# Row blocks of a routed expert layer: one slot per block, loaded four at a time, and the experts' output biases added per batch

## The reference, cut to what matters

```python
sh = gelu(einsum('td,sdh->sth', xf, sW1) + sb1[:, None, :])          # 2 shared experts, hidden 512
shared = (einsum('sth,shd->std', sh, sW2) + sb2[:, None, :]).mean(axis=0)
topk_vals, topk_idx = top_k(xf @ rW + rb, 2)                         # 8 experts, 2 per token
w = sum(softmax(topk_vals)[:, :, None] * onehot(topk_idx), axis=1)   # [token, expert], 0 where not chosen
h = gelu(einsum('td,edh->eth', xf, W1) + b1[:, None, :])
y = einsum('eth,ehd->etd', h, W2) + b2[:, None, :]
return shared + einsum('te,etd->td', w, y)
```

## Time and profile before

| | us |
|---|---|
| median of 3 runs | 788.84 (787.33, 788.84, 797.35) |
| the profiled execution, its time | 788.99 |
| its span in the profile | 786.9 |

### The profile page before, as it was taken

The page is one execution under the profiler, slowest core; times in us unless marked ns, Lnnn a source line. Parts: engine busy times, 40 slices in busy tenths (PEclk is TensorE's granted clock), DMA queues, the critical chain, the costliest instruction groups (busy, mean ns, idle before and its releaser), DMA issues.

```text
span 786.9 us, 10406 instructions
## 1 busy us (share of the span) xinstructions
PE 566.9 (72%) x3665; PEld 404.0 (51%) x3665; DVE 363.1 (46%) x1067; ACT 338.1 (43%) x565; POOL 251.2 (32%) x296
## 2 busy tenths in 40 slices
PE   2654552678788869878699882996987696987770
PEld 2213431455355633656436752765874675776660
DVE  4869279616673465645624571226321240133113
ACT  1186574565737556654475140330322242322220
POOL 3204047202351254311613147113322437033231
PEclk9955665689897989987589996999878788969895
DMA  4400000395000000000000102532161402656632
GB/s 125 147 1 1 1 1 0 82 170 195 1 1 1 15 1 0 1 1 1 1 0 1 55 14 69 154 102 67 39 188 43 135 21 100 190 143 182 200 94 80
DMA packets 37763, 51.60 MB, mean 66 GB/s; under 512 B 7097, under 2 KB 27362, under 8 KB 37442
## 3 DMA queue, kind: packets, MB, share of 16 engines
q1 hardware_dynamic: 35218, 45.82, 20.9%
q0 software_dynamic: 2496, 5.15, 1.8%
HBM read 41.28 MB, written 13.86 MB: 70 GB/s over the span
## 4 chain that ended last, share of the span: by engine, by line
PE 44%; DVE 23%; POOL 7%; DMA 7%; ACT 7%; issue 7%; SPq 5%; POOLq 0%; DVEq 0%; ACTq 0%
SPq L427 5%; PE ring_s L850 4%; PE bank_d L760 4%; PE bank_o L880 3%; PE bank_m L682 3%; PE ring_s L652 3%; PE ring_u L747 3%; PE bank_o L866 3%; PE ring_s L844 2%; DMA token_pairs<-y_blk,x_blk 2%; PE bank_o L669 2%; DMA x_blk<-expert_rows 2%; POOL expert_rows L1150 2%; PE bank_r L546 2%; PE ring_u L739 2%
## 5 line engine op out<-in xcount | busy, mean ns | idle before, releaser
L958 ACT ACTIVATE probs<-ring_s 128x512 f32<-128x512 f32 (+1 forms) x192 | 95.5, 524 | 118.6 <-PE ring_s L652 116.9
L1100 POOL TENSOR_SCALAR_AFFINE_SELECT probs<-probs 128x256 f32<-128x256 f32 (+1 forms) x96 | 51.6, 570 | 178.7 <-ACT probs L964 178.7
L652 PE MATMUL ring_s<-qT,kT 64*128 64x128 bf16 (+3 forms) x256 | 64.2, 350 | 49.4 <-ACT probs L958 37.8
L1013 ACT ACTIVATE g_ring<-ring_s,w_blk 128x128 f32<-128x128 f32 x184 | 52.5, 370 | 104.4 <-PE ring_s L850 95.4
L1161 POOL DMA_INDIRECT token_pairs<-y_blk,x_blk x46 | 45.6, 991 | 143.9 <-DVE y_blk L1672 143.1
L964 ACT ACTIVATE probs<-probs 128x2560 f32<-128x2560 f32 x32 | 74.8, 2337 | 0.8
L652 PEld LDWEIGHTS ring_s<-qT,kT 64*128 64x128 bf16 x256 | 16.4, 97 | 93.4 <-ACT probs L958 58.6
L850 PE MATMUL ring_s<-xT_blk,w_blk 128*128 128x128 f32 x368 | 57.0, 305 | 4.3 <-DVE xT_blk L1665 2.6
L682 PE MATMUL bank_m<-pair_sum,oT 128*128 128x64 f32 x256 | 44.0, 327 | 22.2 <-DVE oT L1467 22.2
L1063 POOL TENSOR_TENSOR rstd<-var_eps,neg_half 128x4 f32<-128x4 f32 x24 | 24.9, 1036 | 100.5 <-DVE var_eps L1394 100.4
L850 PEld LDWEIGHTS ring_s<-xT_blk,w_blk 128*128 128x128 f32 x368 | 53.4, 222 | 6.8 <-issue 4.3
(11 more groups left out here) (356 smaller groups left out, 1076.8 us busy)
## 6 DMA issues: line engine op xcount, KB each, us to landing
w_blk<-expert_pack SPq DMA_DIRECT2D x46, 514.0 KB
expert_pack<-in_L_ffn_W SPq DMA_DIRECT2D x16, 256.0 KB
expert_rows<-blank SPq DMA_DIRECT2D x2, 1560.0 KB, 10.5
x_blk<-expert_rows SPq DMA_DIRECT2D x46, 65.0 KB
y_pair<-token_pairs SPq DMA_DIRECT2D x4, 512.0 KB
x_in<-in_x SPq DMA_DIRECT2D x4, 256.0 KB, 2.9
cosm<-in_c_cos SPq DMA_DIRECT2D x1, 1024.0 KB, 6.8
sin_fwd<-in_c_sin_fwd SPq DMA_DIRECT2D x1, 1024.0 KB, 9.4
```

The lines of the kernel that those rows point to most:

```text
L652: last = mm(bank[:, c:c + w], kT[64 * r:64 * r + 64, p // 2, P * j:P * (j + 1)], qT[64 * r:64 * r + 64, p, P * j:SEQ], start=True, stop=True)
L958: f(probs[:, p % 2, BASE[n]:BASE[n] + WIDTH[n]], ring_s[k % 2][:, 0:WIDTH[n]], ACT.Tanh, scale=1.0 / (CAP * float(np.sqrt(np.float32(HD))) ...
L1013: last = f(g_ring[:, s % RING, P * n:P * (n + 1)], ring_s[s % 2][:, P * n:P * (n + 1)], ACT.Gelu, bias=w_blk[:, k % SLOTS, HID + n:HID + n ...
L1100: last = g.affine_select(out=v, in_=v, compare_op=ALU.is_ge, fill=0.0, base=0, pattern=[[0, v.shape[1]], [1, P]], channel_multiplier=-1)
```

## The change

What it does, in five parts:

1. `x_blk` gets a slot for each of the 23 blocks of a group. The rows of a group are loaded by six DMAs of up to four blocks (`XL = 4`), issued at the start of the group, before the first block's weights. `load_block` keeps only the wait for `u_down`, the read of the table and the load of the weights. At group 1 the loads of rows wait for all sends of group 0.
2. The buffer of weighed results `y_blk` shrinks from 6 slots to 3 (`YS = 3`): `weigh` of block k waits for the send of block k-3.
3. The bias of the experts leaves the blocks: L881 and the load of `b2_blk` go. The transposed weights `wT` of a batch (32 rows, times 2) with two rows of ones are multiplied by `out_bias` (34 x 512, block-diagonal: `b2` four times, and `sb2` four times) in one matmul per batch, in the place of the four of L871. The row for it comes from one PE transpose in `rank`, which so waits for the end of `route` (`w_ready`), and one more DVE instruction in `place`.
4. `out_bias` is filled by 8 small DMAs in the place of the one of `sb2_rows`, ahead of the two loads of blanks, and set to 0 before that by GpSimd.
5. `acc` goes: `settle` and `final` work in `x2`; `settle` waits for the copy of `x2` into the rows (`rows_copied`). `xT` and `sc` change places in SBUF.

```diff
 SLOTS = 6
+YS = 3
+XL = 4
...
-        ones2 = sb("ones2", [NSH, P])
-        sb2_rows = sb("sb2_rows", [NSH, D])
+        out_bias = sb("out_bias", [NT * NE + NSH, NT * D])
...
-            load(sb2_rows[:, :], t["L0_ffn_sb2"], ld_pack)
             sp.wait_ge(blank_ready, 1)
+            for j in range(NT):
+                load(out_bias[NE * j:NE * (j + 1), D * j:D * (j + 1)], t["L0_ffn_b2"], ld_bias)
+                load(out_bias[NT * NE:NT * NE + NSH, D * j:D * (j + 1)], t["L0_ffn_sb2"], ld_bias)
...
                 load(w_blk[:, k % SLOTS, :], pack_dram[bass.ds(e * P, P), :], w_landed[k % SLOTS])
-                load(b2_blk[0:1, k % SLOTS, :], t["L0_ffn_b2"][bass.ds(e, 1), :], w_landed[k % SLOTS])
-                if k >= SLOTS:
-                    sp.wait_ge(y_sent[k % SLOTS], 16 * (k // SLOTS))
-                at = g * GROUP_ROWS + q * P
-                load(x_blk[:, k % SLOTS, :], rows_dram[at:at + P, :], xs_landed[k % SLOTS])
+
+            def load_rows(g, n):
+                m = min(XL, NB - XL * n)
+                at = g * GROUP_ROWS + XL * n * P
+                load(x_blk[:, XL * n:XL * n + m, :], rows_dram[at:at + m * P, :].rearrange("(q p) w -> p q w", p=P), xs_landed[n])
...
+                if g:
+                    for n in range(YS):
+                        sp.wait_ge(y_sent[n], 16 * len(range(n, g * NB, YS)))
+                for n in range(x_loads):
+                    load_rows(g, n)
                 for q in range(NB):
...
-                last.then_inc(rank_ps, 1)
+                pe.wait_ge(w_ready, b + 1)
+                tp(bank_r[0:NT * NE, P:2 * P], of_batch(w_tok_g, b).rearrange("p j e -> p (j e)")).then_inc(rank_ps, 1)
...
-                tp(rows_bank(k)[:, 0:P], x_blk[:, k % SLOTS, 0:D]).then_inc(blk_T, 1)
+                tp(rows_bank(k)[:, 0:P], x_blk[:, k % NB, 0:D]).then_inc(blk_T, 1)
...
-                        pe.wait_ge(ld_pack, 16 * (2 * NE + 2))
-                        for j in range(NT):
-                            last = mm(bank_o[:, P * j:P * (j + 1)], ones2[:, :], sb2_rows[:, :], start=False, stop=(j == NT - 1), skip_group_check=True)
+                        pe.wait_ge(ld_bias, 16 * 2 * NT)
+                        pe.wait_ge(rank_read, of + 1)
+                        last = mm(bank_o[:, :], wT[:, of, :], out_bias[:, :], start=False, stop=True, skip_group_check=True)
...
-                        mm(dst, g[:, P * n:P * (n + 1)], w_blk[:, k % SLOTS, HID + HC + P * n:HID + HC + P * (n + 1)], start=(n == 0), stop=False)
-                    last = mm(dst, ones2[0:1, :], b2_blk[0:1, k % SLOTS, :], start=False, stop=True)
+                        last = mm(dst, g[:, P * n:P * (n + 1)], w_blk[:, k % SLOTS, HID + HC + P * n:HID + HC + P * (n + 1)],
+                                  start=(n == 0), stop=(n == HC - 1))
...
+                op(ts(wT[0:NT * NE, b, :], bank_r[0:NT * NE, P:2 * P], float(NSH), None, ALU.mult))
...
-                if k >= SLOTS:
-                    dve.wait_ge(y_sent[k % SLOTS], 16 * (k // SLOTS))
-                ts(y_blk[:, k % SLOTS, :], down_bank(k)[:, 0:D],
-                   x_blk[:, k % SLOTS, D + 1:D + 2], None, ALU.mult).then_inc(y_ready_blk, 1)
+                if k >= YS:
+                    dve.wait_ge(y_sent[k % YS], 16 * (k // YS))
+                ts(y_blk[:, k % YS, :], down_bank(k)[:, 0:D],
+                   x_blk[:, k % NB, D + 1:D + 2], None, ALU.mult).then_inc(y_ready_blk, 1)
...
-                stt(out=acc[:, b, :], in0=bank_o[:, :], scalar=1.0 / NSH, in1=x2[:, b, :], op0=ALU.mult, op1=ALU.add).then_inc(settled, 1)
+                dve.wait_ge(rows_copied, b + 1)
+                stt(out=x2[:, b, :], in0=bank_o[:, :], scalar=1.0 / NSH, in1=x2[:, b, :], op0=ALU.mult, op1=ALU.add).then_inc(settled, 1)
```

More of the change, by code:

```diff
@@ L311, in build @@
             w_blk = eb("w_blk", [P, SLOTS, PACK])
-            b2_blk = eb("b2_blk", [1, SLOTS, D])
-            x_blk = eb("x_blk", [P, SLOTS, XW])
+            x_blk = eb("x_blk", [P, NB, XW])
             xT_blk = eb("xT_blk", [P, RING, P])
-            y_blk = eb("y_blk", [P, SLOTS, D])
+            y_blk = eb("y_blk", [P, YS, D])
             g_ring = eb("g_ring", [P, RING, SEQ])
@@ L330, in build @@
         rms_tmp = sb("rms_tmp", [P, NT * (NH + NKV)])
+        xT = sb("xT", [P, SEQ])
+        yT = xT
         rms_bits = rms_out[:, :].bitcast(I32)
@@ L360, in build @@
             sem(n) for n in ("ld_attn", "ld_s4", "ld_vec", "ld_cross", "ld_dft", "ld_rest", "ld_wt"))
-        ld_sh, ld_pack, blanked, blank_ready, b1_ready = (sem(n) for n in ("ld_sh", "ld_pack", "blanked", "blank_ready", "b1_ready"))
-        xs_landed = [sem(f"xs_landed{n}") for n in range(SLOTS)]
+        ld_sh, ld_pack, ld_bias, blanked, blank_ready, b1_ready = (sem(n) for n in ("ld_sh", "ld_pack", "ld_bias", "blanked", "blank_ready", "b1_ready"))
+        x_loads = -(-NB // XL)
+        xs_landed = [sem(f"xs_landed{n}") for n in range(x_loads)]
         w_landed = [sem(f"w_landed{n}") for n in range(SLOTS)]
-        y_sent = [sem(f"y_sent{n}") for n in range(SLOTS)]
+        y_sent = [sem(f"y_sent{n}") for n in range(YS)]
         scattered = [sem(f"scattered{g}") for g in range(GROUPS)]
@@ L405, in build @@
             "ff_scaled", "sum_ready", "x2_ready", "x2T_ps", "x2T_sb", "rows_copied"))
-        gates_ps, gates_ready, gates_exp, chosen_ready, rank_ps, rank_read, rows_ready, table_ready = (sem(n) for n in (
-            "gates_ps", "gates_ready", "gates_exp", "chosen_ready", "rank_ps", "rank_read", "rows_ready", "table_ready"))
+        gates_ps, gates_ready, gates_exp, chosen_ready, w_ready, rank_ps, rank_read, rows_ready, table_ready = (sem(n) for n in (
+            "gates_ps", "gates_ready", "gates_exp", "chosen_ready", "w_ready", "rank_ps", "rank_read", "rows_ready", "table_ready"))
         blk_T, blk_xT, u_up, u_gelu, u_down, y_ready_blk, settled = (sem(n) for n in (
@@ L529, in _ @@
                         store(STORE_BEFORE[k])
-                for n in range(SLOTS):
-                    sp.wait_ge(y_sent[n], 16 * len(range(n, (g + 1) * NB, SLOTS)))
+                for n in range(YS):
+                    sp.wait_ge(y_sent[n], 16 * len(range(n, (g + 1) * NB, YS)))
                 for b in range(GB * g, GB * (g + 1)):
@@ L1157, in unit @@
                     if k and k % NB == 0:
-                        for n in range(SLOTS):
-                            pool.wait_ge(y_sent[n], 16 * len(range(n, k, SLOTS)))
+                        for n in range(YS):
+                            pool.wait_ge(y_sent[n], 16 * len(range(n, k, YS)))
                     pool.wait_ge(y_ready_blk, k + 1)
-                    g.indirect_dma_start(out=pair_dram, out_offset=bass.IndirectOffsetOnAxis(ap=x_blk[:, k % SLOTS, D:D + 1].bitcast(I32), axis=0),
-                                         in_=y_blk[:, k % SLOTS, :], in_offset=None).then_inc(y_sent[k % SLOTS], 16)
+                    g.indirect_dma_start(out=pair_dram, out_offset=bass.IndirectOffsetOnAxis(ap=x_blk[:, k % NB, D:D + 1].bitcast(I32), axis=0),
+                                         in_=y_blk[:, k % YS, :], in_offset=None).then_inc(y_sent[k % YS], 16)
             def nothing(*_):
@@ L1604, in route @@
                 one(v.reciprocal(gmax[:, :], gmax[:, :]))
-                one(tt(w_tok, w_tok, gmax[:, :].unsqueeze(2).broadcast_to([P, NT, NE]), ALU.mult))
+                tt(w_tok, w_tok, gmax[:, :].unsqueeze(2).broadcast_to([P, NT, NE]), ALU.mult).then_inc(w_ready, 1)
             def place(b):
```

19 lines of the change are left out of this document (9 added, 10 removed).

## The result

| | us |
|---|---|
| kernel before, 4 runs | 788.09 median (777.71 to 797.35) |
| changed kernel, 4 runs | 747.78 median (740.12 to 758.53) |
| ratio, 95% interval | 0.950 (0.935 to 0.965) |
| profiled execution of the changed kernel | 740.12 (its span 738.1) |

Forecast were 761 us, range 748 to 777: the median lies 13 us lower, at the very edge of the range. Single executions of one kernel are 20 us and more apart here (777.71 to 797.35 above), so the reading goes by stretches, and by two profiles of each kernel. Ratios leave out the executions that were over 1.5% above the fastest of their kernel, while medians are over all of them, so the two can differ by some us.

The account below looks back on a forecast made before the run. No engine bounds the whole; in the blocks TensorE is the bound where rows are in time, and waits 17.1 us for rows. Terms from -15.1 to +2.8 sum to -28.2, taking 789.0 to 760.8: forecast 761 us, range 748 to 777.

Parts of the forecast that it names:

- Biases: Group 0: 23 blocks lose 0.41 us each, the three at the lower clock level 0.73: -10.4 us.
- Clock in group 0: Group 0: a tenth of the 20 us short of full speed goes: -2 us (bounds 0 and -5).
- Waits for rows in group 0: Group 0: three of the 13 waits for rows go, and later weights stay hidden: -4.7 us.
- Group 1: Group 1: -0.85 and -2 us up to the second `final`, then -15.1 from waits for rows, biases and clock.
- Start of group 1: Start of group 1: 1.5 MB of rows ahead of the weights delay the first block: +2.8 us (bounds +1.7 and +14).
- Prologue and `rank`: Seven more small loads ahead of batch 2's input: +2.5 us; the transpose in `rank` and DVE instruction in `place`: +1.6.
- A: Blocks: the weights become the bound, 2.3 us per block at 253 GB/s: +5, 766 us; chance 0.16.
- B: Prologue: all seven small loads wait 2.22 us each, +15.5 instead of +2.5: 774 us; chance 0.09.
- D: Block stages: TensorE's clock falls; at a mean of 0.70, 41 us more: 802 us; chance 0.04.
- E: Blocks: something else released them, gaps stay, only biases go (18 us, less 7 of costs): 778 us; chance 0.06.
- C: Lower clock level vanishes (4 us more), prologue and first weights cost half as much (2.5 us): 754 us; chance 0.13.
- The signs: One rows wait at most, about 3 us for first weights, positions of 2.04 us, batch 2's input 1-4 us later.

Follow-up runs that it names:

- pair: The first profiles of the kernel before and of the changed kernel, side by side; the changed kernel's profiled execution took 740.12 us.
- Each half of the change alone: Against the kernel before: only the biases per batch, 761.32 us (ratio 0.974); only the row slots and loads of four blocks, 763.03 us (0.976).
- full: The changed kernel once more with no edit, for a second profile: 748.33 us, ratio 0.950 to the kernel before.
- split_again: Repeat of the changed kernel with the final norm of batches 0 and 1 cut into four pieces behind four blocks: 739.59 us, ratio 0.943.
- best: The changed kernel with the final norm cut into four pieces and row loads spread between the first weight loads: 739.00 us, ratio 0.939.
- split_final: The changed kernel with the final norm of batches 0 and 1 cut into four pieces behind four blocks: 736.89 us, ratio 0.942.
- ys6: The changed kernel with six slots for weighed results in place of three: 747.78 us, ratio 0.954.

## Why the prediction was right, and where not

The mechanism was right: the waits for rows went, no later wait took their place in full, and the biases counted on TensorE's path. That the sum came as near as it did is in part luck, since its terms were off in both directions. The sizes, by the prediction's own steps, beside the pair and the mean of two profiles of each kernel (three of the biases of group 0 fall into the stretch between the groups, 1.2 us of the forecast):

| stretch | forecast | pair | mean of two |
|---|---|---|---|
| start to the input of batch 2 (prologue) | +2.5 | -1.0 | +1.2 |
| on to the first block of group 0 (`rank`, `place`) | +1.6 | -6.6 | -2.5 |
| group 0, first to last block | -15.9 | -20.4 | -18.7 |
| on to the first block of group 1 (start, three biases) | +1.6 | +0.3 | -0.3 |
| group 1 to the last second matmul | -18.0 | -21.3 | -20.7 |
| the end | 0 | +0.2 | +0.2 |
| sum | -28.2 | -48.8 | -40.8 |

*Biases: too small.* "The bias takes 0.41 us more" was read off the distance between two starts. The position went from 2.46 to 1.90, that is 0.56: with the bias the transpose and the second matmuls beside it shorten their handovers too. Over 46 positions that is 7 us more than forecast, less where TensorE waits anyway. With the clock of group 0, next, this is the largest term that was mis-sized.

*Clock in group 0: too small.* Forecast were 2 us, "a tenth" of the 20. By length times (1 - clock) the stretch was 21.0 and 18.1 us short of full speed before, 10.0 and 12.4 after. That is 6 to 11 us less, a part of it biases that had run at half clock. Each half of the change alone brought it to 10 to 12 as well. That this comes with the change is shown; why either half is enough is not.

*Waits for rows in group 0: not where forecast.* The 4.7 us are gone from the list, but the idle time of the stretch fell by 1.3 us only, and by the second profiles not at all (23.8 and 23.9); TensorE now waits 5.8 us for DVE's `x` where it waited 4.1, and 0.8 for `y_blk` (2.2 in `full`). So of -4.7 us at most -1.3 came. What was gained there came by biases and clock.

*Group 1.* From the second `final` on it was 15.1 forecast, and 46.0 became 30.7 us (717.28 to 763.3, 683.58 to 714.3): 15.3. Before that 2.85 were forecast and 6.0 came (4.6 by the means). That the two waits for rows beside the `final`s "give nothing" was right: what had been 3.1 us of idle time at each place, rows and copy together, is 3.9 now. The forecast that the gaps would be "as long as before" missed that TensorE gets there earlier and DVE does not, so that what a position gains there goes to the gap. The biases of the other positions and the clock were worth more than I gave.

*Start of group 1.* +2.8 forecast for the first block, +2.3 in the pair, +1.7 by the means (7.5 to 9.2). (Its own parts, 6 + 2.1 + 1, add up to 9.1 and +2.6, not to 9.3 and +2.8.) The parts were nearly right: by the estimate above the rows were in some 6.5 us after their issue (forecast 6), and the first block followed some 2.3 us behind them (forecast 3.1). The wait that comes of it was not 3 us before the first block but 1.6, since TensorE had shared work left. The 6.3 us for rows look like a cost of the change and are one in part only: 3.2 of them passed before SP issued the first row load (640.12 to 643.31), while the scatter was still under way. How much of the +2.3 is the loads and how much is where TensorE stood in its shared units, one profile can't say; `split_again` and `best` put up to 2.6 us on the loads. In the stretch as a whole the three biases and the clock pay for it.

The Trainium skill (DMA: Bandwidth & Descriptors, section on the anatomy of one DMA, SWDGE path) has 436 GB/s as the rate in its fit for DMAs that GpSimd issues; by it these loads would take 3.5 us, an estimate. These loads are SP's, and the trace doesn't bear the estimate out: the rows, in pieces of 520 bytes, moved at 243 to 333 GB/s in the single microseconds of three profiles (the first, `full` and `split_again`), and took some 5 us. The weights behind them, in pieces of 4112 bytes, came near the page's rate: 380 to 428 GB/s in the same three.

*Prologue and `rank`: 4.1 us forecast, less to be seen.* The small loads cost 1.8 us at most. The forecast's picture held, that only the first waits for room and that the blanks' waits shrink in return; its "a few hundred bytes" did not (eight or two pieces of 512 bytes each). For `rank` the list of waits shows TensorE held up in two of four batches, 1.5 us together, and the transposes are 0.28 us each: 2.6 us at most. Both are lost in the 16 us by which the unchanged stretch behind them varies. The forecast's own reference was high too: later runs of the kernel before had medians of 780.8 to 783.5 us (11 each), not 789. Against these, 28 us less would have been 753 to 755.

*The rivals.* A, the weights as the bound, is refuted: positions of 1.90 us with one wait of 0.5, and in `best` 285 GB/s without a wait, where A took 253 for the limit. B is refuted by SP's rows: the seven further loads took 0.24 to 0.27 us each, not 2.22. D, a falling clock, is refuted for the blocks: 0.91 and 0.89 after, 0.84 and 0.88 before. E fell with the waits. C (754 us) came nearest, and one of its reasons held: less time at the lower level. The cheaper prologue is too small to be seen, and the largest miss, the price of a bias, is in none of the rivals, so that C came nearest is partly luck too. Its argument, that low stretches begin behind idle time, is borne out in group 1, where `split_final` without the long waits shows a clock of 1.00.

*The signs.* The one wait for rows at the start of group 1 came, L881 is gone, and 51.6 MB were moved by either kernel (not 47). The input of batch 2 was used 1.0 us earlier than 193.36 in the pair and 2.7 us later in `full`, where 1 to 4 later was forecast. No wait of 3 us for the first weights came, and positions are 1.90 us, not 2.04.

## What to carry to other kernels

Price an instruction on a bound engine by the length of a whole position with and without it, not by its own row: here 0.56 us against 0.41. Work of several microseconds on an engine that serves the bound one (DVE's norm ahead of a copy of 0.28 us) is to be cut into pieces that fit between two services; the bound engine gets back the wait, and the stretch at half clock behind it. Where single executions spread by 20 us, take two profiles of either kernel and compare them by stretches, unchanged ones included, before a gain is put down to the change.

## What was not expected of the hardware

In the stretch that the change leaves alone, TensorE's clock is the source of the spread: the same stretch of some 1275 matmul records took from 234.5 to 250.4 us at mean clocks of 0.88 and 0.82, between executions of the same work, and 14 of these 16 us are busy time. In group 0, either half of the change brought the clock from 0.84 and 0.86 to 0.90 and 0.91, although the waits for rows grew in one half and vanished in the other. What sets it there stays open. In group 1 the rows are plainer. The changed kernel and its three variants with the norm in one piece show ten waits of 3.9 us for the copy; behind nine of them TensorE's matmuls ran at half clock for some 3 to 6 us. The tenth, in `ys6`, was as long, and the matmuls behind it ran at full clock: the length of the wait alone does not decide it. With these waits cut out, three profiles show a clock of 1.00, 0.97 and 1.00 (`split_final`, `split_again`, `best`).
